# A sparse graph layer that folds, searches and gathers: adjacency loaded as runs of 2048 columns, the diagonal left in the search

## The reference

```python
h = jnp.maximum(_layernorm(x, axis=-1), 0.0)
mask = adj > 0
head = mask.astype(adj.dtype)
head = head / jnp.maximum(jnp.sqrt(jnp.sum(head * head, axis=-1, keepdims=True)), EPS)
inc = adj + head
edge_fea = inc @ h
edge_degree = jnp.sum(inc, axis=-1, keepdims=True)
return x + edge_fea / edge_degree
```

## Time and profile before

| | |
|---|---|
| median of 3 runs | 1271.77 us (1271.65 to 1273.69) |
| profiled execution, span from first to last instruction | 1276.7 us |
| DVE busy | 1189.2 us, 93% |
| ACT busy | 975.5 us, 76% |
| PE busy | 959.0 us, 75% |
| POOL busy | 791.1 us, 62% |
| moved by the DMA engines | 471.00 MB, mean 369 GB/s |
| mean granted clock of PE | 0.924 |

### The profile page before, as it was taken

The page is one execution under the profiler, slowest core; times in us unless marked ns, Lnnn a source line. Parts: engine busy times, 40 slices in busy tenths (PEclk is TensorE's granted clock), DMA queues, the critical chain, the costliest instruction groups (busy, mean ns, idle before and its releaser), DMA issues.

```text
span 1276.7 us, 14660 instructions
## 1 busy us (share of the span) xinstructions
PE 959.0 (75%) x2680; PEld 478.1 (37%) x2682; DVE 1189.2 (93%) x2868; ACT 975.5 (76%) x1902; POOL 791.1 (62%) x748
## 2 busy tenths in 40 slices
PE   0003878888888878787988887978878888977677
PEld 0001434444444444443434443434444434433343
DVE  6679999998999999998999999999999999999961
ACT  6657787887887988786888877888877888884731
POOL 1003667676666777776766767777776776765562
PEclk9999899898988989899898989999989988987888
DMA  9999999999999999999999999999999999997532
GB/s 356 427 422 406 396 394 388 369 387 369 379 378 382 401 373 401 395 401 394 402 400 401 392 374 384 399 400 395 402 396 402 402 397 373 401 390 275 175 106 74
DMA packets 148207, 471.00 MB, mean 369 GB/s; under 512 B 24826, under 2 KB 24826, under 8 KB 143965
## 3 DMA queue, kind: packets, MB, share of 16 engines
q1 hardware_dynamic: 90368, 331.38, 66.3%
q0 software_dynamic: 57744, 138.64, 29.7%
HBM read 490.47 MB, written 33.82 MB: 411 GB/s over the span
## 4 chain that ended last, share of the span: by engine, by line
DVE 55%; issue 17%; DMA 11%; ACT 6%; PE 6%; another core or an unknown queue 2%; SPq 1%; POOL 0%; DVEq 0%; ACTq 0%; POOLq 0%
DVE cand_word L794 17%; DVE folded L772 16%; DMA adj_tile<-in_adj_dram 8%; DVE cand_index L798 6%; DMA gathered_rows<-in_x_dram 3%; PE acc L1326 3%; DVE cand_index L817 2%; DVE cand_word L812 2%; ACT junk L573 2%; ACT adj_tile L560 2%; ACT diag L636 1%; PE acc L1337 1%; DVE diagonal_alone L779 1%; DVE entry L961 1%
## 5 line engine op out<-in xcount | busy, mean ns | idle before, releaser
L494 POOL DMA_INDIRECT gathered_rows<-h_scratch,slot_column x520 | 559.9, 1077 | 263.1 <-issue 158.0
L573 ACT ACTIVATE junk<-adj_tile,zero_unit 128x2048 bf16<-128x2048 f32 x256 | 510.0, 1998 | 48.3 <-issue 27.5
L1326 PE MATMUL acc<-gathered_rows,diag 128*128 128x512 f32 x1040 | 489.6, 622 | 21.4 <-DMA gathered_rows<-h_scratch,slot_column 18.2
L494 POOL DMA_INDIRECT gathered_rows<-h_scratch,spill_column x198 | 223.1, 1127 | 195.0 <-ACT spill_column L619 135.2
L794 DVE MAX8 cand_word<-folded 128x8 f32<-128x1024 f32 x244 | 298.2, 1222 | 5.9 <-remote 1.3
L772 DVE SCALAR_TENSOR_TENSOR folded<-adj_tile 128x1024 f32<-128x1024 f32 x244 | 296.1, 1214 | 7.7 <-DMA adj_tile<-in_adj_dram 5.6
L1326 PEld LDWEIGHTS acc<-gathered_rows,diag 128*128 128x128 f32 x1040 | 203.8, 204 | 263.4 <-issue 262.6
L798 DVE FIND_INDEX8 cand_index<-cand_word,folded 128x8 uint32<-128x1024 f32 x244 | 297.3, 1219 | 0.0
L1337 PE MATMUL acc<-gathered_rows,spill_matrix 128*128 128x512 f32 x396 | 186.8, 609 | 46.0 <-DMA gathered_rows<-h_scratch,spill_column 42.4
L636 ACT ACTIVATE diag<-ident,weights_and_payload 128x128 f32<-128x128 f32 x581 | 176.2, 388 | 16.0 <-issue 6.5
L1337 PEld LDWEIGHTS acc<-gathered_rows,spill_matrix 128*128 128x128 f32 x396 | 72.8, 192 | 154.8 <-issue 154.6
(11 more groups left out here) (151 smaller groups left out, 880.1 us busy)
## 6 DMA issues: line engine op xcount, KB each, us to landing
adj_tile<-in_adj_dram SPq DMA_DIRECT2D x256, 1024.0 KB
h_scratch<-adj_tile SPq DMA_DIRECT2D x16, 1024.0 KB, 10.6
out_dram<-out_tile SPq DMA_DIRECT2D x64, 256.0 KB
gathered_rows<-in_x_dram SPq DMA_DIRECT2D x12, 1024.0 KB, 12.6
x_residual<-in_x_dram SPq DMA_DIRECT2D x48, 256.0 KB
gathered_rows<-h_scratch,slot_column POOLq DMA_INDIRECT x520
x_held<-in_x_dram SPq DMA_DIRECT2D x4, 1024.0 KB, 7.9
gathered_rows<-h_scratch,spill_column POOLq DMA_INDIRECT x198, 3.5
```

What stands on the lines that cost most here:

```text
L494: nc.gpsimd.indirect_dma_start(out=into, out_offset=None, in_=h[:, :], in_offset=bass.IndirectOffsetOnAxis(ap=column, axis=0), bounds_chec ...
L573: nc.scalar.activation(junk[:, n % 2].rearrange("p (j c) -> p j c", j=2), both[:, :, half], ACT.Relu, bias=zero_unit[:], scale=-UP, accum_ ...
L1326: last = nc.tensor.matmul(acc[t % 3][:], diag[:, t % 2, 1 + s], slot(t % 2, s), start=False, stop=False)
```

## The change

**Loads.** A chunk is now 2048 columns in a row, one run of 8 KB a lane. Its place in SBUF is the same, so fold and check read the same words; the fold pairs column c with c + 1024. The eight parts of the wide tiles then lie in the order of the columns, and the helper part is gone.

**Diagonal.** Read, cut and copy are gone, and with them the wait of SP. The diagonal entry is searched like any other. find_diagonal compares the columns of the eight candidates of its chunk with the known column, and sums the one hit to the first column of val; leave_diagonal subtracts it from its candidate, which so becomes zero. Both need columns_any, which moves up; counts, ranks and columns move behind them. The tests no longer treat right-hand diagonals apart.

**Extra tile.** groups(t) gives 4 groups of spill places for tile 64 too, over two PSUM banks as for tiles 61 to 63.

```diff
-    adj_h = adj.rearrange("(c p j) (h n) -> c j p h n", p=P, j=ROWS, h=2)
+    adj_t = adj.rearrange("(c p j) n -> c j p n", p=P, j=ROWS)
...
         def diag_chunk(t):
-            return t // ROWS * P * ROWS % HALF // CW
+            return t // ROWS * P * ROWS // (2 * CW)
+
+        def diag_column(t):
+            return diag_at[:, t % 16:t % 16 + 1]
...
         def groups(t):
-            return EXTRA if FOLDED <= t < BATCH else FOLDED_EXTRA
+            return EXTRA if wide(t) else FOLDED_EXTRA
...
-                        if j == diag_chunk(t - 2):
-                            sp.wait_ge(diag_read, t - 1)
-                sp.dma_start(chunk(t % 2, j), adj_h[t // ROWS, t % ROWS, :, :, CW * j:CW * (j + 1)]).then_inc(adj_loaded[t % 2][j], 16)
+                sp.dma_start(A[:, t % 2, 2 * CW * j:2 * CW * (j + 1)],
+                             adj_t[t // ROWS, t % ROWS, :, 2 * CW * j:2 * CW * (j + 1)]).then_inc(adj_loaded[t % 2][j], 16)
...
-                if j == diag_chunk(t):
-                    read_diagonal(t)
-                    cut_diagonal(t)
...
-            def keep_diagonal(t):
-                dve.wait_ge(diag_read, min(t, FOLDED - 1) + 1)
-                nc.vector.tensor_copy(val[:, 0:1], on_diag[:, t:t + 1]).then_inc(diag_kept, 1)
+            def in_diag_chunk(ap, t):
+                return ap[:, 0:CAND].rearrange("p (e s) -> p s e", s=CHUNKS)[:, diag_chunk(t)]
+
+            def find_diagonal(t):
+                dve.wait_ge(cola_ready, t + 1)
+                dve.wait_ge(val_ready, t + 1)
+                nc.vector.scalar_tensor_tensor(out=own_entry[:], in0=in_diag_chunk(cola, t), scalar=diag_column(t),
+                                               in1=in_diag_chunk(val[:, 1:], t), op0=ALU.is_equal, op1=ALU.mult,
+                                               accum_out=val[:, 0:1]).then_inc(diag_found, 1)
+
+            def leave_diagonal(t):
+                dve.wait_ge(diag_found, t + 1)
+                rest = in_diag_chunk(val[:, 1:], t)
+                nc.vector.tensor_tensor(rest, rest, own_entry[:], ALU.subtract).then_inc(diag_left, 1)
...
                 if small:
                     values(p)
-                    keep_diagonal(p)
+                    columns_any(p)
                 if pick:
                     find_entry(r)
                 find_places(t, 0)
                 if small:
-                    counts(p)
+                    find_diagonal(p)
                 if pick:
                     take_entry(r)
                 fold(t, 1)
                 if small:
-                    columns_any(p)
-                    ranks(p)
+                    leave_diagonal(p)
                 if pick:
                     sum_entry(r)
                 find_values(t, 1)
                 if small:
+                    counts(p)
+                find_places(t, 1)
+                if small:
+                    ranks(p)
                     columns(p)
-                find_places(t, 1)
                 if small:
                     own_columns(p)
                     pay_columns(p)
```

More of the change, by code:

```diff
@@ L205, in chunk @@
             return A[:, b, 2 * CW * j:2 * CW * (j + 1)].rearrange("p (h c) -> p h c", h=2)
-        def diag_half(t):
-            return t // ROWS * P * ROWS // HALF
         def diag_chunk(t):
-            return t // ROWS * P * ROWS % HALF // CW
-        def diagonal(row, t):
-            first = t // ROWS * P * ROWS % CW
-            return row[:, first:first + P * ROWS].rearrange("p (m j) -> p j m", j=ROWS)[:, t % ROWS]
+            return t // ROWS * P * ROWS // (2 * CW)
+        def diag_column(t):
+            return diag_at[:, t % 16:t % 16 + 1]
         def cands(t):
@@ L283, in add_graph_layer @@
         folded = sem("folded")
-        diag_read = sem("diag_read")
-        diag_cut = sem("diag_cut")
-        diag_kept = sem("diag_kept")
+        diag_found = sem("diag_found")
+        diag_left = sem("diag_left")
         row_ready = sem("row_ready")
@@ L773, in fold @@
                                                op0=ALU.mult, op1=ALU.add).then_inc(folded, 1)
-                if j == diag_chunk(t):
-                    read_diagonal(t)
-                    cut_diagonal(t)
-            def read_diagonal(t):
-                nc.vector.scalar_tensor_tensor(out=picked[:], in0=diagonal(chunk(t % 2, diag_chunk(t))[:, diag_half(t)], t),
-                                               scalar=1.0, in1=ident[:], op0=ALU.mult, op1=ALU.mult,
-                                               accum_out=on_diag[:, t:t + 1]).then_inc(diag_read, 1)
-            def cut_diagonal(t):
-                words = diagonal(F[:, diag_chunk(t) % 2], t)
-                dve.wait_ge(folded, CHUNKS * t + diag_chunk(t) + 1)
-                nc.vector.tensor_tensor(words, words, cap[:], ALU.min).then_inc(diag_cut, 1)
             def find_values(t, j):
                 dve.wait_ge(folded, CHUNKS * t + j + 1)
-                if j == diag_chunk(t):
-                    dve.wait_ge(diag_cut, t + 1)
                 nc.vector.max(out=cv[:, t % 2, 8 * j:8 * j + 8], in_=F[:, j % 2]).then_inc(vals_found, 1)
@@ L801, in part_columns @@
             def part_columns(t, i):
-                if t == BATCH:
-                    return A[:, 0, CW * part(i):CW * (part(i) + 1)]
-                return chunk(t % 2, part(i) % CHUNKS)[:, part(i) // CHUNKS]
+                return A[:, t % 2, CW * i:CW * (i + 1)]
             def part_values(t, i):
@@ L809, in part_values @@
                 else:
-                    dve.wait_ge(adj_loaded[t % 2][part(i) % CHUNKS], 16 * turn(t))
-                e = slice(8 * part(i), 8 * part(i) + 8)
+                    dve.wait_ge(adj_loaded[t % 2][i // 2], 16 * turn(t))
+                e = slice(8 * i, 8 * i + 8)
                 nc.vector.max(out=cv[:, t % 2, e], in_=part_columns(t, i)).then_inc(vals_found, 1)
@@ L864, in columns_any @@
                 dve.wait_ge(idx_found, searched(t) + searches(t))
-                nc.vector.scalar_tensor_tensor(out=ranked(cola[:], t), in0=ranked(ge[:], t), scalar=float(HALF),
+                nc.vector.scalar_tensor_tensor(out=ranked(cola[:], t), in0=ranked(ge[:], t), scalar=float(CW),
                                                in1=by_rank(ci[:, t % 2], t), op0=ALU.mult,
@@ L1035, in count_bad @@
                                                     op0=ALU.mult, op1=ALU.add))
-                step(nc.vector.scalar_tensor_tensor(out=z_right[:, on_right], in0=right_diag[:], scalar=ZERO,
-                                                    in1=z_right[:, on_right], op0=ALU.mult, op1=ALU.add))
                 step(nc.vector.tensor_scalar(well[:], z_left[:], ZERO * HALF, None, ALU.is_equal))
@@ L1077, in wide_period @@
                 values(p)
-                keep_diagonal(p)
+                columns_any(p)
                 part_values(t, 1)
                 find_entry(r)
+                if not wide(p):
+                    find_diagonal(p)
                 part_places(t, 1)
+                if not wide(p):
+                    leave_diagonal(p)
+                take_entry(r)
                 counts(p)
-                take_entry(r)
                 if t == FOLDED + 1:
```

31 lines of the change are left out of this document (11 added, 20 removed).

## The result

| | before | changed |
|---|---|---|
| median of 7 runs each, same chip | 1272.73 us (1271.65 to 1276.63) | 1285.15 us (1274.93 to 1292.4) |
| ratio | | 1.0079, 95% interval 1.0053 to 1.0104 |
| span of the profiled run | 1276.7 us | 1278.5 us (1280.28 with what lies around it) |
| VectorE's tile between like starts, tiles 10 to 60: median, mean | 17.02, 17.30 us | 17.19, 17.41 us |

A forecast was written before the change was run, and what follows sets the result against it. VectorE's own instructions were taken as the bound. Terms -21.4 - 0.7 (count_bad) - 0.2 (wide tiles) + 2.0 = -20.3 us took the median of 1271.77 us to 1251.5 us, range 1242 to 1268.

The forecast's parts named there:

- VectorE's sum: On VectorE, per tile: 0.67 us removed, 0.32 us added, net -0.35 us; for 61 tiles -21.4 us.
- The tail: Extra tile's fourth group on PE: entries +0.68, turning +0.43, last product +0.86 us, together +2.0 us.
- the one under "DMA": Loads on the DMA engines: 403 GB/s needed, the mix could reach 416, so costed at nothing.
- The cover: DMA margin of 13 GB/s: 416 GB/s reachable with 8 KB adjacency runs against 403 needed.
- Rival 1: DMA engines become the bound, 8 KB runs gaining nothing beside gathers: 1261 us, chance 0.13.
- The slower rival: Gathered rows wait behind 8 KB packets, delay returns to VectorE, tile 17.62 us: +21 us, 1292 us, chance 0.12.
- "What is late next": Ranks some 2.4 us and counts some 2.7 us later per tile, PE and ACT waiting for them; costed at nothing.

The follow-up runs named there:

- Run 11: Changed kernel, chunks loaded in two transfers (4 KB packets), each output tile's store cut from 128 rows to 16: 1259.41 us, 0.9801 of the kernel before.
- run 1: Changed kernel, each chunk loaded by two transfers of 1024 columns (4 KB packets), all else as changed: 1273.27 us, 0.9945 of the kernel before.
- run 2: Kernel before with 8 KB runs alone, the diagonal still read and cut: 1283.99 us, 1.0038 of the kernel before.
- run 7: Changed kernel, ScalarE's spill columns ahead of its owner copy and VectorE's ranks early: 1291.54 us in 4 runs, kernel before 1280.66.
- run 5: Changed kernel with VectorE's order altered, counts and ranks early, behind the second fold: 1296.6 us, 1.0126 of the kernel before.
- run 3: Changed kernel with ScalarE's spill columns and spill matrix moved ahead of its owner copy: 1279.12 us, 0.9985 of the kernel before.
- run 4: Changed kernel with TensorE's owner product moved ahead of the spill product: 1288.03 us, 1.0038 of the kernel before.

## Why the prediction was wrong

- **VectorE's sum was right.** find_diagonal 0.14 as taken; columns to own_columns 0.20 against 0.21; the shortest tiles 16.69 us where I had said about 16.7. Run 11 shows the gain in the time once gathers and loads are less late.
- **The tail was right in its terms.** The chain in the tail of the changed kernel, for the earlier trace rows:

```profile
1243.07 1.49 PE pbrought L1279 x4
1244.56 1.12 PE ptr L1279 x4
1245.68 1.71 PE pturned L1285 x8
...
1262.61 6.88 PE acc L1317 x16
```

  The entries cost 2.61 us (+0.56, I had +0.68), turning 1.71 (+0.43), the last product 6.88 (+0.86): +1.85 against +2.0. From the last fold to the end it is 148.1 us, 149.4 before: the tail carries none of the loss.
- **The step that failed is the one under "DMA": "So I cost the loads at nothing, with a cover of 13 GB/s."** It asks only if the loads themselves come in time. They did: folds waited 3.8 us for them, less than before. What the 8 KB packets cost, they cost the other queue: a gather went from 4.8 to 5.9 us, and PE's wait for spill rows from 42.4 to 81.0. I had let this go with "waits of PE cost nothing until they reach DVE"; by the ring they reached it at pay_places, 27.4 us. VectorE's busy time fell by 18.0 us and its idle time among the tiles rose by 19.6, so nothing was left. Runs 1 and 2 show the cause: with the same work and 4 KB packets the ratio is 0.9945 in place of 1.0079, and the 8 KB runs alone cost the kernel before 0.4%.
- **The cover was badly worked out, but it isn't what failed.** I took the efficiency of 8 KB runs from a stretch without gathers and got 416 GB/s for the mix, where 403 were needed. Beside gathers a packet was only 4% quicker a byte by the median (315 against twice 164 ns) and 2% by the mean (324 against twice 166). Yet where VectorE was near its own pace the rate that I needed was there, or nearly. First three tiles of the changed kernel (17.2, 16.7 and 16.7 us), then six of run 7 (16.5 us each):

```profile
489.00:540.00 51.00, 41.98 (x124) 19.89 (x123) 50.27 (x118) 42.36 (x85) 36.35 (x34) 0.97 1.02 406
```
```profile
951.00:1050.00 99.00, 81.54 (x242) 39.79 (x243) 98.59 (x235) 83.50 (x167) 65.65 (x66) 0.97 1.01 401
```

  Rival 1, the DMA engines as the bound, shows in run 1 with its 4 KB packets, not in the changed kernel. Whether the rate would have held for all 61 tiles with 8 KB packets, no run shows.
- **The slower rival was the case**: 8 KB packets, late gathers, a delay that comes back at pay_places (runs 1 and 2); I gave it 0.12. The way back was another than I had said: ACT waits for the owner product, not ahead of row_again. I left out that ACT's spill columns stand behind the owner copy, and PE's owner product behind the spill product, which closes the ring. Its price was too high: +21 us forecast, +12 measured, as not every tile was late: 24 of 61 pay_places waited for ACT. Here the Trainium skill (DMA: Bandwidth & Descriptors, Queues, rings and completion order), by which an engine takes its queues in turn by packet, agrees in direction with 1.1 us more for a gather when the packets between are 8 KB; that they alternate no view shows, nor that what the trace counts as a packet is what that page of the skill calls one.
- **"What is late next" was harmless**, but not for a reason I gave: run 5 moves the ranks back and is slower still. PE waited for the ranks in at most 18 tiles, not in nearly every one.
- The other rule of the Trainium skill that I cited (Perfetto Trace Analysis, DMA Optimizations: longer transfers can raise throughput much where DMA holds a kernel) would have had the time fall; runs 1 and 2 show the longer packets losing here, 1.3% between the changed kernel and run 1 and 0.4% on the kernel before.
- **Still open**: what the rare stops of 1 to 6 us are that came with ACT's and PE's new orders (the profile names no releaser; the kernel before has a few, and some stand at the same place of VectorE's program in two runs, as find_entry at 1011 us in run 3 and at 1014 in run 4); why early ranks cost 0.5% more; and what is left of run 1's waiting folds. Run 11, where loads land 5.6 us sooner with 3% fewer bytes and no earlier request, speaks for the rate, but its mean tile of 17.07 isn't explained by it.

## What to carry to other kernels

A DMA share near 1 tells neither of headroom nor of a bound (it stayed near 1 here with 3% fewer bytes), a mean rate only repeats the length of the tile, and a rate taken from a stretch with one kind of transfer doesn't hold for a mix. Before an engine's saving is booked, ask not only if the loads come in time but which other queue pays for their longer packets. Where small gathers with a deadline share the engines with large loads, keep the loads' packets short: here 4 KB for 8 KB was worth 1.3% (0.9945 against 1.0079). And draw the ring that a late transfer goes round (gather, product, copy, next gather) before costing its wait at nothing: here it took 18 to 20 us, a tile 17. But cutting the ring alone (runs 3 and 4) did not bring the saving.

## What the runs showed of the hardware that I had not expected

- Loads into 64 of the 128 lanes: 230 GB/s at a share of 1.03, 573 ns for an 8 KB packet in place of 315, and the kernel 1.60 times as long.
- 3.1 us without a matmul were followed by a granted clock of 0.50 for 5.5 us; late rows are paid twice on PE.
- Packets of 8 KB gave 4% a byte beside gathers by the median, 2% by the mean, not the 9% of the stretch without them, and slowed each gather by 23% (4.8 to 5.9 us).
